# Layer 2 of a two-layer graph network: one gathered tile in 64 is fetched by SyncE with one-row DMAs instead of by GpSimd

## The reference, cut to what matters

```python
h = jnp.maximum(_layernorm(x, axis=-1), 0.0)
# layer 2, with r = etype[e], norm[e] a scalar weight
H = jnp.einsum('ni,rio->rno', h, W)
msg = (H[etype, src] + b[etype]) * norm
out = jax.ops.segment_sum(msg, dst, num_segments=h.shape[0])
x = x + jax.nn.relu(out)
```

## Time and profile before

| | |
|---|---|
| median of three runs | 8151.24 us (8143.28 to 8152.59) |
| span of the profiled execution, first to last instruction | 8149.0 us |
| layer 2: first to last gather issue of POOL | 4166.5 to 8098.9 us |
| POOL busy in the whole span | 6074.5 us, 75% |
| PE busy in the whole span | 6825.6 us, 84% |

### The profile page before, as it was taken

How to read it: one execution, slowest core, us unless ns; L and a number is a source line. 1 busy time by engine, 2 the same in 40 slices (tenths; PEclk the granted TensorE clock), 3 DMA queues, 4 the chain that set the end, 5 groups by cost and what they waited for, 6 DMA issues and landing times.

```text
span 8149.0 us, 187072 instructions
## 1 busy us (share of the span) xinstructions
PE 6825.6 (84%) x52884; PEld 5276.0 (65%) x52884; DVE 3995.9 (49%) x13480; ACT 1919.9 (24%) x4919; POOL 6074.5 (75%) x6335
## 2 busy tenths in 40 slices
PE   5999999999999999999967777777778877777777
PEld 4666666666666666666646666666666666666665
DVE  7333333333333333333365555555555556555554
ACT  2333333333333333333330000000000000000001
POOL 5777777777777777777757777777777777777776
PEclk7999999999999999999979888888888888988898
DMA  6333333333333333333322222222222222222222
GB/s 141 82 83 82 81 83 82 83 82 83 82 83 82 82 83 82 83 83 82 82 61 53 53 53 53 53 53 52 53 53 53 53 52 53 52 53 53 53 53 72
DMA packets 797549, 566.94 MB, mean 70 GB/s; under 512 B 481443, under 2 KB 671019, under 8 KB 797292
## 3 DMA queue, kind: packets, MB, share of 16 engines
q0 software_dynamic: 200192, 256.65, 14.6%
q1 hardware_dynamic: 597340, 310.10, 14.5%
HBM read 544.45 MB, written 21.68 MB: 69 GB/s over the span
## 4 chain that ended last, share of the span: by engine, by line
PE 32%; issue 24%; POOL 21%; DMA 20%; DVE 1%; POOLq 1%; SPq 0%; ACT 0%; DVEq 0%; ACTq 0%
PE bank L1130 19%; POOL shared L549 17%; DMA shared<-p_tab,idx 11%; DMA rows_place<-h_tab,idx 6%; PE bank L1143 5%; POOL rows_place L549 4%; PE bank L1132 3%; DMA idx<-in_src_t 2%; PE bank L1054 2%; PE bank L1145 1%; PE bank L1061 1%; PE bank L1080 0%; DMA x_in<-in_x 0%; PE bank L1071 0%; DVE stats L744 0%
## 5 line engine op out<-in xcount | busy, mean ns | idle before, releaser
L549 POOL DMA_INDIRECT shared<-p_tab,idx x3128 | 2984.1, 954 | 959.8 <-issue 826.7
L549 POOL DMA_INDIRECT rows_place<-h_tab,idx x3128 | 2978.3, 952 | 964.3 <-issue 804.4
L1130 PE MATMUL bank<-shared,rows_place 128*128 128x256 f32 x6256 | 1842.2, 446 | 860.4 <-issue 748.1
L1130 PEld LDWEIGHTS bank<-shared,rows_place 128*128 128x128 f32 x6256 | 1296.4, 218 | 1126.6 <-issue 782.8
L959 DVE TENSOR_SCALAR shared<-iota_key,key,w_f 128x256 f32<-128x256 f32 x3128 | 1139.1, 425 | 745.3 <-PE bank L1132 633.1
L704 ACT ACTIVATE x_in<-bank 128x256 f32<-128x256 f32 x782 | 300.8, 385 | 3591.9 <-PE bank L1132 3264.7
L1061 PE MATMUL bank<-h_sb,w_tile 128*128 128x128 f32 x6256 | 907.7, 288 | 22.3 <-DVE h_sb L870 0.8
L1061 PEld LDWEIGHTS bank<-h_sb,w_tile 128*128 128x128 f32 x6256 | 758.5, 191 | 232.4 <-DVE h_sb L870 232.1
L1080 PE MATMUL bank<-wn_half,h_sb 128*128 128x128 f32 x6256 | 890.3, 285 | 0.0
L870 DVE TENSOR_SCALAR h_sb<-bank 128x128 f32<-128x128 f32 x782 | 228.2, 292 | 1315.8 <-PE bank L1054 1294.3
L1143 PE MATMUL bank<-x_in,w_rel_sb 128*128 128x64 f32 x6256 | 862.8, 296 | 0.0
(11 more groups left out here) (105 smaller groups left out, 5379.0 us busy)
## 6 DMA issues: line engine op xcount, KB each, us to landing
rows_place<-in_dst_c SPq DMA_DIRECT2D x782, 192.0 KB
shared<-in_edge_cols SPq DMA_DIRECT2D x782, 128.0 KB
shared<-p_tab,idx POOLq DMA_INDIRECT x3128
rows_place<-h_tab,idx POOLq DMA_INDIRECT x3128
idx<-in_src_t SPq DMA_DIRECT2D x1564, 2.0 KB
qr_w<-qr_tab SPq DMA_DIRECT2D x782, 18.0 KB
x_in<-in_x SPq DMA_DIRECT2D x14, 448.0 KB, 4.7
h_tab<-x_in SPq DMA_DIRECT2D x14, 448.0 KB, 3.0
```

The lines of the kernel that those rows point to most:

```text
L549: pool.indirect_dma_start(out=rows_of[s][:, t, :], out_offset=None, in_=table, in_offset=bass.IndirectOffsetOnAxis(ap=idx[s][:, t:t + 1], ...
L1130: pe.matmul(bank[s][:, 0:RW], rows[s][:, t, :], hot_rel[s % 2][:, t, :], start=(t == 0), stop=(t == TC - 1))
```

## The change

SP fetches tile 0 of the chunk at place 13 of every 16 chunks (and of the last 14 chunks, where place 13 is the very last chunk), so 49 tiles of 3128. POOL's gather of those chunks leaves that tile out. SP fetches the tile row by row: for each chunk it passes it loads eight source numbers with one register load, without a range check, and issues eight DMAs of one row of 512 bytes, each to one partition. That is 128 rows in 16 chunks. The rows go to one of two places in `h[0]`, idle in layer 2, and PE's `scatter` reads the tile there. A tile's 128 source numbers are brought to one partition by a DMA of their own at place 5 (`load_ids`), and waited for at place 14 of the 16. Ahead of the first chunk SP loads the numbers of the first such tile, waits for them and issues the first 16 rows (`feed_first`). The loops of layer 2 on SP and POOL now hold 32 chunks in a body, and PE's 16 pairs.

```diff
+    SUP = 16
+    NSUP = NCH // SUP
+    ROWS = P // SUP
+    FED_AT, FED = 13, 1
...
+        fed_rows = h[0][:, 0:2 * FED, :].rearrange("p (k f) d -> p k f d", f=FED)
+        fed_ids = h[0][0:1, 2 * FED:3 * FED, :].rearrange("p f d -> p (f d)").bitcast(i32)
+        fed_ids = [fed_ids, hT[0:1, 0:FED * P].bitcast(i32)]
...
+        def superchunks(eng, m, step):
+            with eng.Fori(0, NSUP // 2) as two:
+                for half in range(2):
+                    for u in range(SUP):
+                        step(Chunk(m, two * (2 * SUP // SL) + (half * SUP + u) // SL, u % SL), u, Lone(m, two, half),
+                             Lone(m, two + half, 1 - half))
+            for u in range(NCH - NSUP * SUP):
+                step(Chunk(m, NSUP * SUP // SL + u // SL, u % SL), u, Lone(m, NSUP // 2, 0), None)
...
+        def feed(eng, f, lone, piece, landed):
+            _, at = nc.values_load_multi_w_load_instructions(
+                fed_ids[lone.half][0:1, f * P + piece * ROWS:f * P + (piece + 1) * ROWS], engines=(eng.engine,),
+                min_val=0, max_val=NPAD - 1, skip_runtime_bounds_check_because="a source node's number is below the number of nodes")
+            for k, row in enumerate(at):
+                p = piece * ROWS + k
+                eng.dma_start(fed_rows[p:p + 1, lone.half, f, :], h_tab[ds(row, 1), :]).then_inc(landed[lone.half], 16)
+
+        def feed_step(eng, f, lead, u, lone, after, landed):
+            first = FED_AT - lead - SUP + 1
+            if u - first < SUP:
+                feed(eng, f, lone, u - first, landed)
+            elif after:
+                if u == first + SUP:
+                    eng.wait_ge(fed_ids_landed, 16 * after.ids_turn + 16)
+                    hold(eng)
+                feed(eng, f, after, u - first - SUP, landed)
+
+        def feed_first(eng, f, lead, m, landed):
+            eng.wait_ge(fed_ids_landed, 16 * Lone(m, 0, 0).ids_turn + 16)
+            hold(eng)
+            for piece in range(SUP - 1 - FED_AT + lead):
+                feed(eng, f, Lone(m, 0, 0), piece, landed)
...
             def layer1_pass(m):
-                def step(c):
+                def load_ids(lone):
+                    sp.dma_start(fed_ids[lone.half], src_t[:, ds((lone.k * SUP + FED_AT) * TC, FED)].rearrange("p o -> o p"),
+                                 allow_slow_non_contiguous=True).then_inc(fed_ids_landed, 16)
+
+                def step(c, u, lone, after):
                     s = c.slot
                     sp.wait_ge(scattered[s], c.turn + 1)
                     hold(sp)
                     sp.dma_start(idx[s][:, :], src_t[:, ds(c.i * TC, TC)]).then_inc(idx1_landed[s], 16)
-
-                all_chunks(sp, m, step)
+                    if u == 5 and after:
+                        load_ids(after)
+                    feed_step(sp, 0, 0, u, lone, after, sp_row_landed)
+
+                load_ids(Lone(m, 0, 0))
+                feed_first(sp, 0, 0, m, sp_row_landed)
+                superchunks(sp, m, step)
...
+            def step1(c, u, lone, after):
+                gather(c, h_tab, rows, scattered, idx1_landed, rows_landed, range(FED if u == FED_AT else 0, TC))
+
             with pool.Fori(0, passes) as m:
-                all_chunks(pool, m, lambda c: gather(c, h_tab, rows, scattered, idx1_landed, rows_landed))
+                superchunks(pool, m, step1)
...
-                pe.wait_ge(rows_landed[s], 16 * TC * c.turn + 16 * TC)
+                pe.wait_ge(rows_landed[s], 16 * tiles_gathered(c, u, lone))
+                if u == FED_AT:
+                    pe.wait_ge(sp_row_landed[lone.half], 16 * P * lone.turn + 16 * P)
                 pe.wait_ge(sums_copied[s], c.turn + 1)
                 for t in range(TC):
-                    pe.matmul(bank[s][:, 0:RW], rows[s][:, t, :], hot_rel[s % 2][:, t, :], start=(t == 0), stop=(t == TC - 1))
+                    there = fed_rows[:, lone.half, t, :] if u == FED_AT and t < FED else rows[s][:, t, :]
+                    pe.matmul(bank[s][:, 0:RW], there, hot_rel[s % 2][:, t, :], start=(t == 0), stop=(t == TC - 1))
```

More of the change, by code:

```diff
@@ L233, in gnn_two_layers @@
         pass1_ready, pass1_step = sem("pass1_ready"), sem("pass1_step")
+        fed_ids_landed, sp_row_landed = sem("fed_ids_landed"), slot_sems("sp_row_landed", 2)
         block = ctx.enter_context(nc.Block())
@@ L297, in paired, with __init__ @@
             step(None, at(NPAIR - 1), None)
+        assert NSUP % 2 == 0 and NCH == NSUP * SUP + FED_AT + 1
+        LONE_USES = [NSUP // 2 + 1, NSUP // 2]
+        class Lone:
+            def __init__(self, m, two, half):
+                self.m, self.half = m, half
+                self.k = two * 2 + half
+                self.turn = m * LONE_USES[half] + two
+                self.ids_turn = m * (NSUP + 1) + self.k
+        def superchunks(eng, m, step):
[6 more added lines that the diff above has]
+                step(Chunk(m, NSUP * SUP // SL + u // SL, u % SL), u, Lone(m, NSUP // 2, 0), None)
@@ new lines, in tiles_gathered @@
+        def tiles_gathered(c, u, lone):
+            if c.slot != FED_AT % SL:
+                return TC * c.turn + TC
+            return (c.m * (TC * SLOT_USES[c.slot] - FED * (NSUP + 1)) + lone.k * (TC * SUP // SL - FED)
+                    + (TC * (u // SL + 1) - FED * (u >= FED_AT)))
+        def feed(eng, f, lone, piece, landed):
[5 more added lines that the diff above has]
+                eng.dma_start(fed_rows[p:p + 1, lone.half, f, :], h_tab[ds(row, 1), :]).then_inc(landed[lone.half], 16)
@@ L540, in _, with gather @@
             pool.iota(pass_i[:, :], [[W, MAXPASS]], base=0, channel_multiplier=0).then_inc(ramps_set, 1)
-            def gather(c, table, rows_of, used, idx_there, landed):
+            def gather(c, table, rows_of, used, idx_there, landed, tiles=range(TC)):
                 s = c.slot
@@ L547, in gather @@
                 hold(pool)
-                for t in range(TC):
+                for t in tiles:
                     pool.indirect_dma_start(
@@ L1119, in _, with scatter @@
             all_groups(pe, lambda k: transpose_agg(k, k.it, mid_added))
-            def scatter(c):
+            def scatter(c, u, lone):
                 s = c.slot
                 pe.wait_ge(hot1_built[s], c.turn + 1)
-                pe.wait_ge(rows_landed[s], 16 * TC * c.turn + 16 * TC)
+                pe.wait_ge(rows_landed[s], 16 * tiles_gathered(c, u, lone))
+                if u == FED_AT:
+                    pe.wait_ge(sp_row_landed[lone.half], 16 * P * lone.turn + 16 * P)
                 pe.wait_ge(sums_copied[s], c.turn + 1)
                 for t in range(TC):
-                    pe.matmul(bank[s][:, 0:RW], rows[s][:, t, :], hot_rel[s % 2][:, t, :], start=(t == 0), stop=(t == TC - 1))
+                    there = fed_rows[:, lone.half, t, :] if u == FED_AT and t < FED else rows[s][:, t, :]
+                    pe.matmul(bank[s][:, 0:RW], there, hot_rel[s % 2][:, t, :], start=(t == 0), stop=(t == TC - 1))
                 for t in range(TC):
@@ L1146, in project, with step1 @@
                   .then_inc(projected[p.half], 1)
-            def step1(pair, before, after):
+            def step1(pair, before, u, lone):
                 if pair:
-                    for c in pair.chunks:
-                        scatter(c)
+                    for k, c in enumerate(pair.chunks):
+                        scatter(c, u + k, lone)
                 if before:
                     project(before)
+            PAIRS = SUP // 2
             with pe.Fori(0, passes) as m:
-                paired(m, pe, step1)
+                at = lambda i, two=0: Pair(m, two * PAIRS + i // 2, i % 2)
+                step1(at(0), None, 0, Lone(m, 0, 0))
+                with pe.Fori(0, NSUP // 2) as two:
+                    for i in range(1, 2 * PAIRS + 1):
+                        ahead, half, u = i // (2 * PAIRS), i // PAIRS % 2, i % PAIRS * 2
+                        step1(at(i, two), at(i - 1, two), u, Lone(m, two + ahead, half))
+                for i in range(NSUP * PAIRS + 1, NPAIR):
+                    step1(at(i), at(i - 1), (i - NSUP * PAIRS) * 2, Lone(m, NSUP // 2, 0))
+                step1(None, at(NPAIR - 1), None, None)
             all_groups(pe, lambda k: transpose_agg(k, k.it + NG // 2, (fin_even, fin_relu)))
```

## The result

The changed kernel took 8136.5 us (median of 15 runs, 8132.72 to 8148.51) against 8150.47 us for the kernel before on the same chips (15 runs). The ratio is 0.9984, with a 95% interval of 0.9976 to 0.9991. So it is faster, by 14 us or 0.16%, where 51 us or 0.63% were forecast. The time lies inside the range of 8086 to 8300 us, but the size is off by more than a factor of three.

The account below looks back on a forecast made before the run. POOL's gathers were taken to bound layer 2, with SP 96% full. 8149.0 - 61.6 for gathers left out + 10.3 for the start gave 8097.7 us of span, 8100 us as median, 0.63% faster; range 8086 to 8300 us.

Parts of the forecast that it names:

- What bounds the kernel before: Layer 2: POOL sets the pace and waits for nobody, one gather in 1.2576 us, 5.03 us for a chunk.
- What leaves POOL: Layer 2: 49 gathers left out, each giving its whole step of 1.2576 us, 61.6 us in all.
- The start: Ahead of layer 2's first chunk: fetching numbers and issuing 16 rows makes everything behind start 10.3 us later.
- A row on SP: SP in layer 2: register arithmetic, move, gaps and issue of one row DMA, 0.42 us, 3.36 us for eight.
- The register load: SP in layer 2: eight numbers in one load for each chunk, 0.65 us, with a gap 0.70 us.
- S: Time SP needs for a layer 2 chunk: 4.73 us against POOL's 4.95 us, a margin of 0.22 us.
- the part for `idx`: SP's earlier work for each layer 2 chunk, semaphore, arithmetic, move, DMA issue and gaps: 0.57 us.
- `load_ids` with its wait and the loop arithmetic: SP in layer 2: `load_ids` once in 16 chunks, wait, hold and loop arithmetic, 0.10 us a chunk at most.
- SP becomes the bound: Rival: above 4.95 us a chunk SP sets layer 2's time, 8151.2 + 10.3 - 3933 + 782 x S; slower, chance 0.22.
- no change: Rival: POOL's longer layer 2 loop costs what it saves, 47 us lost, 8147 us; chance 0.10.
- SP just at POOL's pace: Second way to no change, beside the loop, sharing its chance of 0.10; no size of its own.
- the 1.95 us that were named for POOL: Possible stop at each of 24 ways back of POOL's layer 2 loop, from an unexplained gap at the layer's start.

Follow-up runs that it names:

- e5: Changed kernel with SP's part of layer 2 written out, no loop on SP: 8105.0 us, ratio 0.9936 to the kernel before the change.
- e10: Changed kernel with 16 row numbers per register load in every second chunk, SP's loop kept: 8088.31 us, ratio 0.9935 to the kernel before.
- e16: Changed kernel with SP's layer 2 written out and 16 row numbers per load: 8087.07 us, ratio 0.9931 to the kernel before.
- e12: Changed kernel without SP's feeding, 32-chunk loops kept, POOL gathering all 3128 tiles: 8138.05 us, ratio 0.9999 to the kernel before.
- e1: Changed kernel with 128 instead of 32 chunks in SP's layer 2 loop body, on a slow chip: ratio 1.0538 to the kernel before.
- e17: Changed kernel with two more empty instructions in SP's queue for each chunk, on a slow chip: ratio 1.0524 to the kernel before.
- e9: Changed kernel without SP's feeding, long loops kept, POOL gathering all tiles, on a slow chip: 11669.77 us, ratio 0.9975 to the kernel before.

## Why the prediction was wrong, point by point

- **What bounds the kernel before**: right. POOL's pace is the floor, and e5, e10 and e16 all end there, at 0.64 to 0.69% faster. That agrees with the forecast of 0.63%. The view of the chain that ended last could have misled here: from 4200 to 8080 us it puts 39.4% of the kernel before on PE's L1130 and 7.7% on POOL's gather. The gather's longest wait of 0.3 us decided rightly, since leaving out 49 gathers paid in full once SP kept up.
- **What leaves POOL**, 61.6 us: right in kind and size for a kernel in which SP keeps up. e10, for instance, has 1.2549 us from gather to gather.
- **The start**: 10.3 us forecast, 10.5 measured.
- **A row on SP**: 0.42 us forecast. Measured are 0.037 + 0.029 + 0.228 and three gaps, 0.41 us from issue to issue. The choice of L437 as the nearest row was right.
- **The register load**: 0.65 us forecast, 0.716 measured.
- **S, the step that failed.** The sum of what SP needs for a chunk was 4.73 us against a measured 4.996, a difference of 0.27 us where the margin was 0.22. The largest part was put at nothing: the stops that SP's long body brought. In 23 rounds (736 chunks) there are 23 stops of 2.62 us at the way back, 0.082 us for a chunk, and 184 stops of 0.35 us within the code, 0.087 us for a chunk. Less the ordinary gap between two instructions, which was in the sum, that is 0.16 us. The other 0.11 us is made up of small terms: the register load 0.07, the part for `idx` 0.05, `load_ids` with its wait and the loop arithmetic 0.03, less 0.04 on the eight rows. Neither part alone exceeds the margin: with the stops and nothing else S would be 4.89, with the small terms and nothing else 4.84. The prediction had the stop at the way back in hand, and let it go with the sentence "On PE and SP the same stop would be covered by idle time". It had just shown that SP has 4% of idle time left. The stop was weighed for POOL, where it cost nothing (e12), and not added to S.
- **The rivals.** "SP becomes the bound" was the mechanism, and its formula gives the measured time to 1.5 us when S = 4.996 is put in; so close a hit is partly luck, as the 15 runs spread over 16 us. The chance of 0.10 for no change had "SP just at POOL's pace" as one of its two ways; that is nearly what happened. A trace of before could not show the stops, since SP's body there has 20 instructions. Had the 1.95 us that were named for POOL been put on SP's way back, S would have been 4.73 + 1.95 / 32 = 4.79, still under 4.95: that would have shown how thin the margin was, not that it was gone.
- **The range**: two of its bounds don't follow from the reasons given. 0.2% below 8100 is 8084 and not 8086, and a start twice as long gives 8110 and not 8115. Nothing hangs on either.
- The Trainium skill ("Runtime: NRT & Kernel Launch", section "Instruction fetch mechanics") says that a taken branch to code outside two pages of instructions stops for a fetch. The trace agrees: SP's body of 956 instructions stops for 2.62 us, POOL's of 224 doesn't. The same section's figure of about 200 ns for each register is not borne out by these loads, which read SBUF: one value took 0.432 us, eight 0.716 and 16 in e10 1.164, which is 0.041 to 0.056 us for each further value.

Shown by runs: that SP's queue was the bound (e5, e10), that POOL's floor ends the gain (e16), and that the long bodies of POOL and PE cost nothing by themselves (e12). Shown by the traces as going together: SP's stops and the loads of code. In the kernel after every stop has its packet on the instruction queue; in e5 the way back is gone and with it the long stops, while those of 0.35 us remain, each with its packet; in e12, with a short body on SP, there are neither stops nor more than four packets. No run changed the loading of code and nothing else, so that it is the cause of the stops is argued. Worked out from the trace and not measured by a run of its own: how much of the loss is the stop at the way back alone.

## What to carry to other kernels

When work is moved to a queue that is nearly full, write down the whole round of its loop, with the way back and what the loop's length does to it, and compare the two rounds: here 159.9 us against 158.5. A stop that was free on an idle engine is charged in full once that engine sets the pace, and removing any of its work then helps, not only the stop. Leave such a queue more than a few per cent of room: e10 and e16 gain four times as much as the change for a few lines of code. And a kernel without the moved work tests a long loop only where the body stays long without it.

## What the runs showed of the hardware that was not expected

- SP's DMA of one row of 512 bytes to one partition took 0.228 us to issue, 0.41 us with its register work and gaps, against 0.33 to 0.36 for one to 128 partitions. 6272 of them left POOL's step from gather to gather as it was: 1.2549 us with them (e10), 1.2550 without (e12, the same chip).
- A register load took 0.432 us for one value, 0.716 us for 8 and 1.164 us for 16, far from proportional.
- SP's straight code, too, had a stop: 0.35 us at every 128th instruction, about 1 us ahead of an 8 KB packet on the instruction queue.
- The slow chips. There the kernel before took 11679 to 11933 us. Chips 6 and 13 were slow in some runs and normal in others (e1 and e16; e17 and e5). Data instructions of POOL, DVE and ACT were not slower. PE's were: in the kernel of e9 and e12 the matmuls of L1152 took 353 ns instead of 285 on average, at a mean granted clock of 0.755 instead of 0.933. Sequencer instructions were slower now and then. In e17, from 9000 to 9500 us, the move ahead of a row's DMA has the same median as ever and a maximum near 1.4 us:

```profile
L343 SPq MOVE h<-h_tab x546: 2/29/1395, 9000.1 to 9498.4; - x182
```

and POOL waits several us for `idx` (start, us, what, idle time ahead):

```profile
9013.69 0.94 POOL L624 DMA_INDIRECT rows_place<-h_tab,idx  x1 [0.30 <-issue]
9019.53 1.11 POOL L624 DMA_INDIRECT rows_place<-h_tab,idx  x1 [4.89 <-DMA idx<-in_src_t]
```

The kernels in which SP's queue is nearly full lost the most there. That it is these stretched instructions which cost them the 3 to 6% was not tested, and what makes a chip slow was not found out.
